# Window attention with graph experts: the first residual added by accumulating transfers, three tasks moved between slots, the sort spread by a new table

## The chip, the cores and the metric

The kernel runs on one core of a Trainium2 chip. A core has engines that run their own instruction queues side by side and wait for each other through semaphores: TensorE (PE, matrix multiply), VectorE (DVE), ScalarE (ACT), GpSimd (POOL) and SyncE (SP, which here only issues transfers). The metric is the time of one execution on the device in microseconds (us), the median of a few runs. Lower is better.

## What is computed

```python
# x: 32 images of 32x32 tokens x 128 features, float32
y = window_attention(layernorm(x))            # 8x8 windows, 8 heads, no mask
y = roll(window_attention(roll(y, (-4, -4)), shift_mask), (4, 4))   # same weights
x = x + y                                      # the residual of this document
t = layernorm(x)                               # 32768 tokens
h = t @ W_gat                                  # 16 graph features a token
# graph attention over 524288 random edges plus one loop a token: a softmax over
# each token's incoming edges gives the scores of 4 experts, the best 2 are taken
out = x + sum_over_top2(gate[e] * (gelu(t @ W1[e] + b1[e]) @ W2[e] + b2[e]))
```

The edges have to be sorted by destination, which the kernel does itself, with compare-and-exchange operations on VectorE over 557,056 keys that lie in SBUF.

## The kernel before

There are three stages, one after the other: `attention` (both window attentions, the layer norm of the result, the graph features, and the whole sort), `edges` (gathers of graph features and the experts), `combine` (gates and sum). Only `attention` is touched.

**Steps and slots.** `attention` is a software pipeline written out by hand. A step is one image for each of two streams: A, the first attention, of image n, and B, the second, of image n-2. There are 39 steps from -2 to 36; streams run in steps 0 to 33. A step has eight slots, one for each pair of windows. In a slot TensorE computes the scores of its pair (lines 929 and 934, by `scores`), transposes those of two slots ago (L948, `turn`), weighs the values of three slots ago (L963, `weigh`), and then does the slot's tasks. It may start the scores of a slot only after VectorE has subtracted the maximum in the slot before (`s_sub`). VectorE takes maximum and subtraction (L1155, L1157, `less_maximum`), then a number of sort operations (L1072 and L1077, smaller and larger), then perhaps statistics of a layer norm (L1061) or a reciprocal (L1145).

**Tasks.** `SLOT_TASKS` lists them by slot. Av/Bv, Ak/Bk and Aq/Bq are value, key and query projections of the streams, FT and CT transposes of normalised images, Ao/Bo transposes of attended values, CH the graph features (L898), and CZ0 and CZ1 the two halves of the result x + attention. `LAG` says how many steps later a task comes for its image. Each task fills one of two PSUM banks (`misc`), taken in turn; ScalarE empties it by a copy. TensorE must wait (`s_free`) until the task two before has been emptied.

**The result.** `result` on TensorE adds three things in the bank: the output bias (one bf16 matmul, L875), the residual `xres` through the identity (L876, 512 columns in float32, shown as one instruction in the program and two in the trace), and attended values times `wo` (L880). ScalarE copies the bank to `x2` (L696). SP loads `xres` once a step (L503) and stores `x2` (L516). VectorE takes the statistics of `x2` in slot 7 (L1061), GpSimd makes mean and deviation of them in 15 linked small instructions (`deviation(1)`, L571 to L585), ScalarE normalises (L738).

**GpSimd** multiplies attended values by the reciprocals of their sums (L601, `normalised_output`) in every second slot, does `deviation(0)` for the input image in slot 4 and `deviation(1)` in slot 7.

**The sort** is one generator of 739 operations. `place_sort` hands them to slots by a credit: `spare(slot)` is what a slot of 7.8 us has left on VectorE after a fixed part, of which the last term comes from a table of eight numbers, one a slot. When a part of the keys has to be transposed, `place_sort` puts turn pieces (tasks S, L911 on TensorE, up to two in a slot, each a bank of 512 or 256 columns) into the slots that follow.

Of the kernel before, what the change touches and what calls it, by code (L numbers as in the profile page):

```python
# [25 lines left out]
P = 128  # L26
# [229 lines left out]
def attention(nc, x, w_qkv, b_qkv, w_o, b_o, w_gat, att_src, att_dst, edge_index, x2_out, tnT_out, node_rows, sorted_keys):  # L256
# [8 lines left out]
    with ExitStack() as ctx:  # L265
# [6 lines left out]
        def sem(name):  # L272
# [24 lines left out]
        xres = sb("xres", [P, TILES, P])  # L297
# [36 lines left out]
        s_xres = sem("s_xres")  # L334
# [35 lines left out]
                      ["CH0", "CZ0"],  # L370
                      ["Bk0", "Bq0", "CZ1"],
# [7 lines left out]
        def spare(slot):  # L379
            k, j = divmod(slot, PAIRS)  # L380
            n = k + FIRST_STEP
            if n < 0:
                return 3.0 if n == -1 and j > 0 else 0.0
            two = LAG["B"] <= n < IMAGES
            busy = (2.5 if two else 1.5) + 0.8
            busy += (0.7, 0.7, 0.7, 0.7, 3.6, -0.6, -0.9, 1.7)[j]
            return SLOT_US - (0.0 if two else 1.5) - busy
# [52 lines left out]
        def _(sp):  # L440
# [49 lines left out]
            for n in steps:  # L490
# [6 lines left out]
                if active("CZ0", n):  # L497
                    m = n - LAG["CZ0"]
                    if m > 0:

                        wait_full(sp, "CZ0", m - 1)
                        wait_full(sp, "CZ1", m - 1)
                    sp.dma_start(xres[:, :, :], x[m].rearrange("(j r) c d -> (r c) j d", j=TILES)).then_inc(s_xres, 16)  # L503
                if active("Ak0", n):
                    own_rows("A", n - LAG["Ak0"], 0)
                if active("CH0", n):
# [3 lines left out]
                if active("Bk0", n):  # L510
                    own_rows("B", n - LAG["Bk0"], 0)
                if active("CZ0", n):
                    m = n - LAG["CZ0"]
                    wait_free(sp, "CZ0", m)
                    wait_free(sp, "CZ1", m)
# [15 lines left out]
        def _(pool):  # L531
# [54 lines left out]

            def normalised_output(n, j):
# [16 lines left out]
            for n in steps:  # L604
                for j in range(PAIRS):
# [3 lines left out]
                    if j == 4 and 0 <= n + 2 < IMAGES:  # L609
                        deviation(0, n + 2)  # L610
                    if j == 7 and active("CZ0", n):
                        deviation(1, n - LAG["CZ0"])
# [199 lines left out]
        def _(pe):  # L812
# [55 lines left out]
            def result(n, task):  # L868
# [5 lines left out]
                pe.wait_ge(s_xres, 16 * m + 16)  # L874
                pe.matmul(t[:, :], all_ones[:, :], osplit[:, :, :].rearrange("p j d -> p (j d)"), start=True, stop=False)  # L875
                pe.matmul(t[:, :], ident[:, :], xres[:, 4 * i:4 * i + 4, :].rearrange("p j d -> p (j d)"), start=False, stop=False)  # L876
# [113 lines left out]
        def _(dve):  # L990
# [169 lines left out]
            for n in steps:  # L1160
                for j in range(PAIRS):
# [14 lines left out]
                    if j == 7 and active("CZ0", n):  # L1176
                        for i in range(2):
                            wait_free(dve, f"CZ{i}", n - LAG["CZ0"])
                        statistics(1, x2, range(TILES), n - LAG["CZ0"])
# [824 lines left out]
```

## Time and profile before

| | |
|---|---|
| time, median of 3 runs | 7,803.55 us (7,803.08 to 7,804.34) |
| the profiled execution | 7,804.57 us, span of its records 7,803.0 us |
| busy over the span | PE 50%, DVE 62%, ACT 27%, POOL 65% |
| mean granted TensorE clock | 0.717 of full speed |
| busy in the attention stage's slices | PE and DVE about nine tenths |

The busy time of an engine is the time in which it executes; waiting for a semaphore is not in it. The shares over the span mix stages: GpSimd leads with the gathers of the second stage, which the change does not touch. Times in the rows below are microseconds from the start of the span. A name such as `attn_keys<-attn_keys` is what is written and what is read, with buffer numbers left out, so that `attn_x` stands for `x2`. An operation of 128x512 in float32 on TensorE appears as two instructions. What ended an idle time stands behind "<-".

### The profile page before, as it was taken

What the parts mean: (1) busy time and instruction counts of PE and PEld (TensorE: products, weight loads), DVE (VectorE), ACT (ScalarE), POOL (GpSimd) and SP (SyncE); (2) the same over time, 40 slices, a digit from 0 to 9 for tenths busy, and PEclk for the clock granted to TensorE, in tenths of its full rate; (3) what the DMA queues carried; (4) which work ended last, traced back from release to release, by engine and by line L of the source; (5) the groups of instructions that cost most, each with busy time, mean ns of one, the idle gap of its engine ahead of it and who ended that gap; (6) DMA issues with size and microseconds to landing.
All of it is one profiled execution on the core that took longest, in us unless ns stands there. A gap on an engine that the chain in (4) does not pass through costs nothing. (4 is left out here: it accounts for less than half of the span.)

```text
span 7803.0 us, 90796 instructions
## 1 busy us (share of the span) xinstructions
PE 3918.8 (50%) x32089; PEld 2498.6 (32%) x32216; DVE 4873.7 (62%) x6373; ACT 2140.2 (27%) x4195; POOL 5082.2 (65%) x5738
## 2 busy tenths in 40 slices
PE   5999999996333433433343343334334333433347
PEld 3666666665212221221222122122212212221123
DVE  9999899997545544554554455455445545544568
ACT  4888888885111111111111111111111111111000
POOL 5443333333777777777777777777777777777674
PEclk9999999998666666666666666666666666666578
DMA  1222222222111211111121111111112111111188
GB/s 51 58 64 57 59 61 60 62 60 71 34 33 33 44 33 33 39 38 33 33 44 33 33 41 36 33 37 40 33 33 44 33 33 39 38 33 33 34 255 278
DMA packets 503676, 417.71 MB, mean 54 GB/s; under 512 B 160546, under 2 KB 400338, under 8 KB 502866
## 3 DMA queue, kind: packets, MB, share of 16 engines
q1 hardware_dynamic: 355842, 356.89, 14.6%
q0 software_dynamic: 147552, 56.96, 7.5%
q8 instruction: 190, 3.11, 0.2%
q14 instruction: 92, 0.75, 0.0%
HBM read 203.44 MB, written 176.45 MB: 49 GB/s over the span
## 5 line engine op out<-in xcount | busy, mean ns | idle before, releaser
L1648 POOL DMA_INDIRECT edge_G<-node_rows,edge_src x4352 | 4126.5, 948 | 1326.3 <-issue 1326.3
L1703 PE MATMUL edge_hbank<-edge_xt,edge_w 128*128 128x512 f32 x1024 | 719.7, 859 | 2755.5 <-ACT edge_hid L1673 2739.5
L1452 DVE TENSOR_TENSOR edge_oh<-edge_wbank,edge_dlf 128x3072 bf16<-128x3072 f32 x512 | 1682.8, 3349 | 62.3 <-PE edge_cbank L1728 46.9
L1409 DVE COPY edge_O<-edge_O 128x24 f32<-128x24 f32 x64 | 12.5, 195 | 2344.7 <-DMA edge_G<-node_rows,edge_src 2344.7
L1703 PEld LDWEIGHTS edge_hbank<-edge_xt,edge_w 128*128 128x128 f32 x1024 | 254.8, 275 | 3184.7 <-ACT edge_hid L1673 3029.3
L1683 ACT ACTIVATE edge_w<-edge_w 128x272 f32<-128x272 f32 x64 | 27.5, 429 | 4043.4 <-DVE edge_w L1423 4043.4
L1728 PE MATMUL edge_cbank<-edge_oh 128*128 128x256 bf16 x4096 | 803.6, 366 | 649.4 <-DVE edge_oh L1452 649.1
L1728 PEld LDWEIGHTS edge_cbank<-edge_oh 128*128 128x128 bf16 x4096 | 477.2, 125 | 952.0 <-DVE edge_oh L1452 814.6
L601 POOL TENSOR_TENSOR attn_att<-attn_oraw,attn_rsum 128x512 f32<-128x512 f32 (+1 forms) x136 | 138.9, 1022 | 952.2 <-DVE attn_rsum L1145 900.3
L1072 DVE TENSOR_TENSOR attn_keys<-attn_keys 128x1024 f32<-128x1024 f32 (+1 forms) x340 | 478.4, 1407 | 9.8
L1077 DVE TENSOR_TENSOR attn_keys<-attn_keys 128x1024 f32<-128x1024 f32 (+1 forms) x340 | 476.8, 1402 | 0.1
L1717 PE MATMUL edge_ybank<-edge_w,edge_hid 128*128 128x128 f32 x4096 | 474.4, 277 | 0.0
L1717 PEld LDWEIGHTS edge_ybank<-edge_w,edge_hid 128*128 128x128 f32 x4096 | 462.2, 192 | 26.1 <-ACT edge_hid L1673 26.1
L1673 ACT ACTIVATE edge_hid<-edge_hbank,edge_b1c 128x512 f32<-128x512 f32 x512 | 344.8, 686 | 255.1 <-PE edge_hbank L1703 254.4
L1155 DVE TENSOR_REDUCE attn_mx<-attn_score 128x16 f32<-128x1024 f32 (+1 forms) x272 | 308.8, 1135 | 106.6 <-PE attn_score L934 67.6
L1157 DVE TENSOR_TENSOR attn_S<-attn_score,attn_mx 128x1024 f32<-128x1024 f32 (+1 forms) x272 | 315.9, 1162 | 9.4
L1845 PE MATMUL comb_total<-comb_ye,comb_ident 128*128 128x512 f32 x512 | 238.8, 630 | 160.5 <-DVE comb_ye L1939 81.8
L929 PE MATMUL attn_score<-attn_km,attn_qT 64*64 64x256 f32 x4096 | 291.9, 399 | 44.5 <-DVE attn_S L1157 35.8
L792 ACT ACTIVATE attn_pT<-attn_turn 128x1024 f32<-128x1024 f32 (+1 forms) x272 | 273.6, 1006 | 93.0 <-PE attn_turn L948 91.6
L963 PE MATMUL attn_out<-attn_vx,attn_pT 128*64 128x34 f32 x8192 | 293.3, 226 | 0.1
L1862 POOL DMA_INDIRECT comb_srow<-state_rows,end_index x256 | 242.1, 946 | 78.1 <-issue 78.1
L948 PE MATMUL attn_turn<-attn_ident,attn_S 128*128 128x128 f32 x2048 | 288.6, 283 | 1.8 <-ACT attn_pT L792 1.8
(282 smaller groups left out, 6465.1 us busy)
## 6 DMA issues: line engine op xcount, KB each, us to landing
edge_G<-node_rows,edge_src POOLq DMA_INDIRECT x4352, 2.4
expert_out<-edge_yo SPq DMA_DIRECT2D x64, 1024.0 KB, 4.3
comb_ye<-expert_out SPq DMA_DIRECT2D x32, 2048.0 KB, 13.6
state_rows<-edge_O SPq DMA_DIRECT2D x64, 816.0 KB
attn_km<-attn_kT SPq DMA_DIRECT2D x1024, 32.0 KB, 2.0
attn_xin<-in_x SPq DMA_DIRECT2D x32, 512.0 KB, 4.3
attn_xres<-in_x SPq DMA_DIRECT2D x32, 512.0 KB, 5.4
x_rows<-attn_x SPq DMA_DIRECT2D x32, 512.0 KB, 3.4
```

The costliest lines, as they stand in the source:

```text
L929: last = pe.matmul(out[2 * e + a], qT[st][h][halves[a], w * WTOK:(w + 1) * WTOK], km[st][halves[a], h, :, w, :], start=True, stop=mask[e] ...
L963: last = pe.matmul(out_bank[e * WTOK:(e + 1) * WTOK, j % OUT_SLOTS, c:c + VW], pT[j % 2][:, st, g, e * WTOK:(e + 1) * WTOK], vx[st][:, 2 * ...
L1072: return dve.tensor_tensor(out, a, b, ALU.min)
L1077: return dve.tensor_tensor(out, a, b, ALU.max)
L1155: dve.tensor_reduce(top, scores, AX_X, ALU.max).then_inc(s_mx, 1)
L1157: dve.tensor_tensor(S[j % RING_S][:, :, lo:hi, :, :].rearrange("p a s h k -> p a (s h) k"), scores, top.unsqueeze(3).to_broadcast([P, 2, ( ...
L1452: dve.tensor_tensor(oh[:, r:r + WIDE, :, :].rearrange("p t k n -> p (t k) n"), iota.unsqueeze(1).to_broadcast([P, 3 * WIDE, P]), dlf[:, t: ...
L1648: pool.indirect_dma_start(G[b][:, t, :], None, node_rows, bass.IndirectOffsetOnAxis(ap=src[b][:, t:t + 1], axis=0)).then_inc(s_g[b][2 * t ...
L1673: act.activation(hid[:, k, :], hbank[k % 2][:, :], ACT.Gelu, bias=b1c[:, k:k + 1]).then_inc(s_ge, 1)
L1703: pe.matmul(hbank[k % 2][:, :], w1[:, k // HB, (k % HB) * P:(k % HB + 1) * P], xt[b][:, :], start=True, stop=True).then_inc(s_l1, 1)
L1717: last = pe.matmul(ybank[:, t, x * P:(x + 1) * P], hid[:, x * HB + h, t * P:(t + 1) * P], w2[:, x, h, :], start=False, stop=(x == EXPERTS ...
L1728: pe.matmul(cbank[:, 0:HI], oh[:, t % RING, 0, :], oh[:, t % RING, 1:3, :].rearrange("p k n -> p (k n)"), start=(t == 0), stop=(t == HC - ...
```

## The change

1. TensorE no longer adds the residual. ScalarE copies bias and projection to `x2` as before; then GpSimd issues two transfers a step, one for each half (`add_residual`, slot 5), that read the image and add it to what stands in `x2` (`accum_op`). VectorE's statistics and SP's store wait for both (`s_added`). `xres` and its load are gone.
2. Slot 5 has Bk0, CZ0, CZ1 (before: CH0, CZ0), slot 6 has Bq0, CH0 (before: Bk0, Bq0, CZ1). SP's transfers follow.
3. The table of `spare` has new numbers.

```diff
-                      ["CH0", "CZ0"],
-                      ["Bk0", "Bq0", "CZ1"],
+                      ["Bk0", "CZ0", "CZ1"],
+                      ["Bq0", "CH0"],
...
-            busy += (0.7, 0.7, 0.7, 0.7, 3.6, -0.6, -0.9, 1.7)[j]
+            busy += (0.85, -0.1, 0.05, 0.2, 3.05, -0.5, 0.55, 2.4)[j]
...
-                    sp.dma_start(xres[:, :, :], x[m].rearrange("(j r) c d -> (r c) j d", j=TILES)).then_inc(s_xres, 16)
                 if active("Ak0", n):
                     own_rows("A", n - LAG["Ak0"], 0)
+                if active("Bk0", n):
+                    own_rows("B", n - LAG["Bk0"], 0)
...
                 if active("CZ0", n):
                     m = n - LAG["CZ0"]
-                    wait_free(sp, "CZ0", m)
-                    wait_free(sp, "CZ1", m)
+                    sp.wait_ge(s_added, 32 * m + 32)
                     sp.dma_start(x2_out[m].rearrange("(j p) d -> p j d", p=P), x2[:, :, :]).then_inc(s_x2st, 16)
...
+            def add_residual(m):
+                rows = x[m].rearrange("(j r) c d -> (r c) j d", j=TILES)
+                for i in range(2):
+                    wait_free(pool, f"CZ{i}", m)
+                    half = slice(TILES // 2 * i, TILES // 2 * (i + 1))
+                    pool.dma_start(x2[:, half, :], rows[:, half, :], accum_op=ALU.add).then_inc(s_added, 16)
...
+                    if j == 5 and active("CZ0", n):
+                        add_residual(n - LAG["CZ0"])
...
-                pe.wait_ge(s_xres, 16 * m + 16)
                 pe.matmul(t[:, :], all_ones[:, :], osplit[:, :, :].rearrange("p j d -> p (j d)"), start=True, stop=False)
-                pe.matmul(t[:, :], ident[:, :], xres[:, 4 * i:4 * i + 4, :].rearrange("p j d -> p (j d)"), start=False, stop=False)
...
-                        for i in range(2):
-                            wait_free(dve, f"CZ{i}", n - LAG["CZ0"])
-                        statistics(1, x2, range(TILES), n - LAG["CZ0"])
+                        m = n - LAG["CZ0"]
+                        dve.wait_ge(s_added, 32 * m + 32)
+                        statistics(1, x2, range(TILES), m)
```

TensorE, slot 5 and the tasks of slot 6 in step 18, before (the score, turn and weigh rows of slot 6 left out; L911 are turn pieces, lines after the change are two lower):

```order
L898 MATMUL attn_misc<-attn_wgat,attn_tnT 128x24 x8
L875 MATMUL attn_misc<-attn_osplit,attn_all_ones 128x512
L876 MATMUL attn_misc<-attn_xres,attn_ident 128x512
L880 MATMUL attn_misc<-attn_wo,attn_attB 128x128 x4
L911 MATMUL attn_misc<-attn_ident,attn_keys 128x128 x8
...
L844 MATMUL attn_misc<-attn_ywin,attn_wfold 128x512 x2
L875 MATMUL attn_misc<-attn_osplit,attn_all_ones 128x512
L876 MATMUL attn_misc<-attn_xres,attn_ident 128x512
L880 MATMUL attn_misc<-attn_wo,attn_attB 128x128 x4
```

and after, the same tasks of slots 5 and 6:

```order
L844 MATMUL attn_misc<-attn_ywin,attn_wfold 128x512
L874 MATMUL attn_misc<-attn_osplit,attn_all_ones 128x512
L878 MATMUL attn_misc<-attn_wo,attn_attB 128x128 x4
L874 MATMUL attn_misc<-attn_osplit,attn_all_ones 128x512
L878 MATMUL attn_misc<-attn_wo,attn_attB 128x128 x4
...
L844 MATMUL attn_misc<-attn_ywin,attn_wfold 128x512
L896 MATMUL attn_misc<-attn_wgat,attn_tnT 128x24 x8
```

The graph features left slot 5 for slot 6, one key projection and the second half of the result went the other way, and the residual is gone; the turn pieces of this step stand in slots 0, 4 and 5 before and in 0, 3 and 4 after.

VectorE, slot 6 of step 18, before (keys are the sort):

```order
L1155 TENSOR_REDUCE attn_mx<-attn_score 128x16
L1157 TENSOR_TENSOR attn_S<-attn_score,attn_mx 128x1024
L1072 TENSOR_TENSOR attn_keys<-attn_keys 128x128x8
L1077 TENSOR_TENSOR attn_keys<-attn_keys 128x128x8
L1072 TENSOR_TENSOR attn_keys<-attn_keys 128x256x4
L1077 TENSOR_TENSOR attn_keys<-attn_keys 128x256x4
L1072 TENSOR_TENSOR attn_keys<-attn_keys 128x512x2
L1145 RECIPROCAL attn_rsum<-attn_oraw 128x32
```

and after:

```order
L1153 TENSOR_REDUCE attn_mx<-attn_score 128x16
L1155 TENSOR_TENSOR attn_S<-attn_score,attn_mx 128x1024
L1075 TENSOR_TENSOR attn_keys<-attn_keys 128x256x4
L1070 TENSOR_TENSOR attn_keys<-attn_keys 128x512x2
L1075 TENSOR_TENSOR attn_keys<-attn_keys 128x512x2
L1143 RECIPROCAL attn_rsum<-attn_oraw 128x32
```

Three sort operations stand in the slot instead of five; slots 1 and 3 have one more each.

GpSimd, from the end of `deviation(0)` in a step to the start of `deviation(1)`, after:

```order
L576 TENSOR_TENSOR attn_nw<-attn_nw 128x8 [waits attn_s_dev]
L583 DMA attn_x<-in_x 128x4x128 [waits attn_s_free1]
L583 DMA attn_x<-in_x 128x4x128 [waits attn_s_free0]
L599 TENSOR_TENSOR attn_att<-attn_oraw,attn_rsum 128x512 [waits attn_s_recip,attn_s_oc]
L562 TENSOR_TENSOR attn_nw<-attn_st 128x8 [waits attn_s_momentc]
```

The two transfers are new; the multiplication of slot 6 (L599, L601 before) now stands behind them.

## Rows read from the trace of the kernel before

**Rows 1.** Windows: stretch, length, busy (count) by engine, granted clock, DMA share, GB/s.

```profile
144.40:557.80 413.40, 374.44 (x5257) 266.16 (x5272) 406.21 (x391) 331.02 (x749) 180.41 (x252) 0.98 0.22 59
557.80:1788.60 1230.80, 1130.53 (x15398) 812.91 (x15444) 1114.43 (x1290) 1011.85 (x2310) 401.81 (x709) 1.00 0.22 59
1881.90:1916.90 35.00, 18.67 (x87) 15.32 (x87) 16.80 (x32) 12.18 (x32) 5.76 (x16) 0.60 0.35 118
```

**Rows 2.** Waits of DVE, 557.8 to 1788.6: total us, times, longest.

```profile
DVE attn_mx L1155 <- PE attn_score L934: 65.3, 44, 4.8
DVE attn_mx L1155 <- PE attn_score L929: 36.7, 26, 5.0
```

**Rows 3.** Timeline of PE, 1016 to 1079: start, length, operation, count, idle before.

```profile
1017.44 1.09 PE L929 MATMUL attn_score<-attn_km,attn_qT 64*64 64x256 f32 x16
...
1050.76 1.23 PE L911 MATMUL attn_misc<-attn_ident,attn_keys 128*128 128x128 f32 x8 [1.58 <-ACT attn_kT L646]
1051.92 1.09 PE L929 MATMUL attn_score<-attn_km,attn_qT 64*64 64x256 f32 x16
...
1057.16 1.02 PE L876 MATMUL attn_misc<-attn_xres,attn_ident 128*128 128x512 f32 x2
1058.02 1.05 PE L880 MATMUL attn_misc<-attn_wo,attn_attB 128*128 128x128 f32 x8
1058.91 0.60 PE L911 MATMUL attn_misc<-attn_ident,attn_keys 128*128 128x128 f32 x4
...
1060.35 1.09 PE L929 MATMUL attn_score<-attn_km,attn_qT 64*64 64x256 f32 x16
...
1067.53 1.09 PE L929 MATMUL attn_score<-attn_km,attn_qT 64*64 64x256 f32 x16
...
1073.16 1.09 PE L929 MATMUL attn_score<-attn_km,attn_qT 64*64 64x256 f32 x16
```

**Rows 4.** Groups by line, PE, 557.8 to 1788.6: busy us, mean ns, idle before.

```profile
L911 PE MATMUL attn_misc<-attn_ident,attn_keys 128*128 128x128 f32 x536 | 85.8, 284 | 52.3 <-ACT attn_vx L656 15.2 <-ACT attn_ywin L684 13.2 <-ACT attn_attB L675 9.6
...
L876 PE MATMUL attn_misc<-attn_xres,attn_ident 128*128 128x512 f32 x88 | 44.9, 592 | 4.5
```

**Rows 5.** Timeline of DVE, 1052 to 1079.

```profile
1053.17 1.22 DVE L1155 TENSOR_REDUCE attn_mx<-attn_score 128x16 f32<-128x1024 f32 x1 [2.15 <-PE attn_score L934]
...
1055.57 1.22 DVE L1072 TENSOR_TENSOR attn_keys<-attn_keys 128x1024 f32<-128x1024 f32 x1
...
1059.10 1.22 DVE L1077 TENSOR_TENSOR attn_keys<-attn_keys 128x1024 f32<-128x1024 f32 x1
...
1074.91 1.64 DVE L1061 BATCH_NORM_STATS2 attn_st<-attn_x 128x6 f32<-128x128 f32 x8
```

**Rows 6.** Timeline of POOL, end of deviation(0) in step 18.

```profile
1059.37 1.00 POOL L584 TENSOR_TENSOR attn_nw<-attn_nw 128x8 f32<-128x8 f32 x1
1060.45 0.20 POOL L585 TENSOR_TENSOR attn_nw<-attn_nw 128x8 f32<-128x8 f32 x1
```

**Rows 7.** Line L1648, gathers of the second stage: durations, and issue to landing.

```profile
L1648 POOL DMA_INDIRECT edge_G<-node_rows,edge_src x4352: 940/944/1505, 1923.8 to 7375.3; - x198
...
DMA to landing us min/median/max: 2.2/2.4/3.3
```

**Rows 8.** DMA issues, 400 to 1600: count, KB each, median us to landing.

```profile
attn_xin<-in_x SPq DMA_DIRECT2D x22, 512.0 KB, 4.4
attn_xres<-in_x SPq DMA_DIRECT2D x22, 512.0 KB, 5.4
```

**Rows 9.** Timelines of ACT, PE, DVE and POOL, end of the stage.

```profile
1883.48 3.20 ACT L738 ACTIVATE attn_normed<-attn_x,attn_nw 128x128 f32<-128x128 f32 x8
...
1883.41 3.61 PE L898 MATMUL attn_misc<-attn_wgat,attn_tnT 128*128 128x24 f32 x16 [1.11 <-ACT attn_attB L675]
...
1893.81 1.64 DVE L1061 BATCH_NORM_STATS2 attn_st<-attn_x 128x6 f32<-128x128 f32 x8 [1.22 <-ACT attn_x L696]
...
1916.86 0.19 POOL L1621 IOTA edge_posi<- 128x68 int32 x1 [14.78 <-POOLq L265]
```

More of the change, by code:

```diff
@@ L296, in attention @@
         normed = sb("normed", [P, TILES, P])
-        xres = sb("xres", [P, TILES, P])
         x2 = sb("x2", [P, TILES, P])
@@ L333, in attention @@
         s_xin = sem("s_xin")
-        s_xres = sem("s_xres")
+        s_added = sem("s_added")
         s_xn = sem("s_xn")
@@ L496, in _ @@
                     load_x(n + 2)
[L497 to L502, printed above, removed]
-                    sp.dma_start(xres[:, :, :], x[m].rearrange("(j r) c d -> (r c) j d", j=TILES)).then_inc(s_xres, 16)
                 if active("Ak0", n):
                     own_rows("A", n - LAG["Ak0"], 0)
+                if active("Bk0", n):
+                    own_rows("B", n - LAG["Bk0"], 0)
                 if active("CH0", n):
@@ L509, in _ @@
                     sp.dma_start(node_rows[m].rearrange("(j p) d -> p j d", p=P), hrow[:, :, :]).then_inc(s_hst, 16)
-                if active("Bk0", n):
-                    own_rows("B", n - LAG["Bk0"], 0)
                 if active("CZ0", n):
                     m = n - LAG["CZ0"]
-                    wait_free(sp, "CZ0", m)
-                    wait_free(sp, "CZ1", m)
+                    sp.wait_ge(s_added, 32 * m + 32)
                     sp.dma_start(x2_out[m].rearrange("(j p) d -> p j d", p=P), x2[:, :, :]).then_inc(s_x2st, 16)
```

## The prediction

> **What bounds the kernel now.** I read the page first: its strip of TensorE is nearly full up to the slice in which the second stage starts, at 1916.86 [rows 9], and a third full from there on. The attention stage is all that the change touches. Then the windows, cut at step borders. In steps 2 to 9 VectorE is busy 406.2 of 413.4 us; in steps 10 to 31 (1,230.8 us) it is busy 1,114.4 and TensorE 1,130.5, at a granted clock of 1.00, the 2.4 GHz level [rows 1]. The waits say who is last. In steps 10 to 31 VectorE stands idle 65.3 + 36.7 = 102 us in 70 of 176 slots, each time for scores [rows 2]. So the early steps are VectorE's, and in the later ones TensorE sets the end of many slots, by 102/22 = 4.6 us a step.
>
> Last the timeline of TensorE in step 18. A slot runs from one group of scores to the next: slot 5 is 1051.92 to 1060.35 = 8.4 us, slot 6 7.2, slot 7 5.6, and the eight from 1017.44 to 1073.16 add to 55.7 [rows 3]. TensorE queues its slot in order (scores, turn, weigh, tasks, turn pieces of the sort), so every microsecond in a task list delays the next scores. Turn pieces (L911) also wait for ScalarE to empty the bank before: the 536 transposes cost 85.8 us busy and 52.3 us idle [rows 4]. A pair in slot 4 of step 18 took 1.23 us and waited 1.58 ahead, 2.8 in all; the one in slot 5 took 1060.35 - 1058.91 = 1.4 [rows 3].
>
> **The change, part by part.**
>
> *Residual matmuls out.* From the start of L876 to that of L880 is 1058.02 - 1057.16 = 0.86 us [rows 3]. There are 88 such instructions, two to a task, in the 22 steps [rows 4]: 44 x 0.86 = 37.8 us off TensorE's queue, and the wait of 4.5 us before them can go too. Upper end of the gain: 42 us. In steps 2 to 9 the same saving (8 x 1.7) lies beside VectorE's work and brings 0.
>
> *Tasks moved.* Bk0 to slot 5, CH0 to slot 6, CZ1 to slot 5. The moved work is unchanged; only the slot sums change. With the base part that a slot has anyway, slot 5 goes from 7.1 to 6.5 us and slot 6 from 7.2 to 6.2 (without turn pieces), since a key projection takes 1.0, the graph features 2.0, a result without its residual 1.1. CZ1 needs the bank of Bk0, which ScalarE can empty only after its four normalisations; by the order of ScalarE in the timeline that is at about the moment TensorE arrives, so I count no wait; if the cover is gone it is 0.3 us a step, 7 us.
>
> *Sort spread anew.* Both programs run 739 sort operations. A steady step has 24 before and after: 3,3,3,3,1,4,5,2 by slot before, 3,4,3,4,1,4,3,2 in step 18 after. One costs (1059.10 - 1055.57)/3 = 1.18 us [rows 5]. VectorE's own sum in a step stays at 51 us, so the spread alone is no gain. It moves the turn pieces: the 67 pairs in steps 10 to 31 stay 67, but 15 of them now fall into slot 4 (8 before) and 10 into slot 3 (6 before), where a pair costs up to the 2.8 us, against 1.4 in slots 5 and 6. I put +4 us on it.
>
> *What VectorE takes back.* I laid both engines side by side slot by slot: scores may not start before the subtraction of the slot before, the maximum not before the scores. In step 18 TensorE's slots add to 55.7 us before (7.3, 6.5, 7.1, 5.8, 7.8, 8.4, 7.2, 5.6) and 54.3 after (7.3, 6.5, 7.1, 8.5, 6.5, 6.5, 6.2, 5.6), VectorE's to 51: 1.4 gained. Thirteen of the 22 steps look like this and give 20 us; in the other nine turn pieces cross a step border or VectorE is later, and they add up to 5. The same working, done for the kernel before, gives 1,224 against the 1,231 of the trace. So -25 us, between 0 (VectorE takes all) and -42.
>
> *The accumulating transfers.* The trace has none, so I bound them. GpSimd issues two per step behind deviation(0), whose last link ends at 1060.45 + 0.2 = 1060.7 in step 18 [rows 6]. In the new order both results are emptied by about 1059.3 (7.4 us behind the scores at 1051.92), so GpSimd is the later one. Issue: a gather of 128 rows holds it for 0.94 us [rows 7]; a half has 512 rows of 512 bytes, by rows four times that, 3.8 us. Landing: 2.4 us for a gather [rows 7], 4.4 and 5.4 us for the plain 512 KB loads of xin and xres [rows 8]; for adding, which reads both sides, at most twice the 5.4. I take 1.2 us per issue and 5.4 to land, from the row that moves the same bytes: the second half is issued at 1061.9 and in at 1067.3. Who waits: VectorE for its statistics in slot 7, which stood at 1074.91 [rows 5]; by its own work alone (slot 5: 7.0, slot 6: 6.3, then 2.4 and two sort operations, from 1053.17) it comes there at 1071.2. Slack 3.9 us, cost 0. With both upper ends (issues end 1064.8 and 1068.9, landing 10.8 later) it is in at 1079.7, some 8 us late. Behind the waiting VectorE stand the next maximum and, one slot on, TensorE's scores. Behind GpSimd's issues stands only the multiplication of slot 6, whose reciprocal comes at about 1065. SP's store of x2 waits too; it stood at 1071 or later anyway, and Bk0's key rows leave SP a slot earlier.
>
> One row bears on GpSimd's pace here: a link of deviation(0) takes 1.00 us where the next takes 0.20 [rows 6], beside sort operations on VectorE. The Trainium skill (SBUF — State Buffer, Who interferes with whom) says that a VectorE instruction with two SBUF inputs contends with a GpSimd instruction that reads SBUF, not with one that only writes it, and infers that descriptor writing is therefore spared. By that rule the issues keep to the price of the gathers; were they held as the reads are, each would wait up to one sort operation, 1.2 us, inside the slack. For the landing only a page has a price: the Trainium skill (DMA: Bandwidth & Descriptors, Anatomy of one DMA — SWDGE (gpsimd) path) gives 2.0 us plus bytes at 436 GB/s for a transfer from GpSimd, an estimate of 2.6 us for 256 KB; by it the half would be in at 1064.5 and the sum the same.
>
> *The end of the stage.* The last image has no cover. Before, its statistics wait for the result copy until 1893.81 and everything up to 1916.86 follows in a chain [rows 9]. After, the graph features (3.61 us from 1883.41, the granted clock being 0.60 in this stretch [rows 1]) stand behind the results and the residual is out, but ScalarE's normalisations until 1886.7 [rows 9] stay in front; both results are then copied by about 1888.9, and with 1.2 + 5.4 us the sum lands near 1895.5. +1 us, between -2 and +12.
>
> Sum: the profiled execution took 7,804.6 us with a span of 7,803.0, and the median of three is 7,803.6, so it stands for them. 7,804.6 - 25 + 1 = 7,780 us.
>
> **Rivals.** (a) *VectorE and the turn pieces take it all back.* For it: VectorE is idle in only 70 of 176 slots [rows 2], and the new table puts 4 operations in slots 1 to 3, where TensorE's tasks are short; a pair in slot 4 waits for ScalarE. With the old TensorE lengths the new spread alone costs 6 us by the working above; if slots 5 and 6 come out 0.5 us longer than I have them, the gain is 4 us. Gain of 0 to 15: 7,790 to 7,805. Against: a wait is 102/70 = 1.5 us long on average, three times that 0.5. (b) *The adding transfer lands late: slower.* Place: VectorE's wait before the x2 statistics. It decides from a landing of 1071.2 - 1061.9 = 9.3 us behind the second issue. At 12 us it is 2.7 late in each of 31 steps; TensorE's remaining lead hides about 1, so 31 x 1.7 = +53, less 25, and 5 at the end: 7,837. At the bound of 8 us late it would be over +150. For it: rows of 512 bytes, reads on both sides, and an issue that may cost 3.8 us. Against: a same-sized plain load needs half of 9.3. (c) *All of it shows*, also ScalarE's shorter waits: -40, 7,764. For it: VectorE's idle time of 4.6 us a step leaves room for all of it.
>
> **How the numbers follow.** Forecast 7,780 (its own range 7,768 to 7,790) 0.50; (c) 0.14; (a) 0.20; (b) 0.16. What this kernel's measurement can tell from no change is about 0.2%, 15.6 us. Below 7,788 lie most of the forecast, all of (c): faster 0.63. Same: the rest of it, (a) and a tenth of (b): 0.23. Slower 0.14. The range takes in (c) and the near part of (b): 7,755 to 7,815.
>
> **What would show it.** Right: the L876 group gone, steps 10 to 31 about 1,206 us, VectorE's wait for scores near 75 us, steps 2 to 9 unchanged, a statistics line (L1059) without idle time. Wrong: idle time before L1059 with the DMA as releaser (b); two slots 3 and 4 longer than 8.5 and 6.5 us (a); DMA landings over 9 us.

## The result, and the profile after

The changed kernel takes 7,827.9 us, median of 9 runs (7,821.5 to 7,830.0); beside it on the same chip the kernel before took 7,803.6 (9 runs). The ratio is 1.0027, 95% interval 1.0016 to 1.0037: slower by 0.27%, where I had forecast 0.3% faster. The profiled execution of after took 7,830.0 us with a span of 7,828.3, against 7,804.6 and 7,803.0 before.

I cut both traces at the first maximum (VectorE, L1153, L1155 before) of each step, and do so for every kernel below. All times are us. "Mult" is where GpSimd's multiplication of slot 6 (L599, L601 before) ends, counted from the start of slot 4, the mean of steps 3 to 9. The ratio is to the kernel before, on the same chip, with its interval. The runs stand on three chips: the kernel before takes 7,803.6 us on that of e1 to e4, 7,812.7 on that of e5 to e8 and 7,813.8 on that of e9 to e12, so times in us compare within these groups, and the ratios across them. Stretches of this stage move less: e7, whose ratio is 1.0001, has 413.4 and 1,230.5 us on the second chip where before has 413.3 and 1,230.8.

```
kernel                      steps 0-1   2-9   10-31   32-33   mult   ratio
before                         76.5   413.3  1230.8    74.2   21.7   1
after                          79.9   441.9  1219.5    76.3   24.6   1.0027 [1.0016, 1.0037]
issues in the chain (e1)       81.2   422.1  1211.9    76.3   22.3   0.9991 [0.9982, 1.0001]
nobody waits (e2)              81.3   444.8  1212.4    76.3   24.8   1.0025 [1.0014, 1.0036]
slots and table only (e3)      81.2   417.1  1235.7    76.8   21.3   1.0020 [1.0010, 1.0029]
after, old table (e4)          76.4   444.8  1219.7    73.7   25.6   1.0027 [1.0017, 1.0036]
nobody waits, issued
  behind the mult (e5)         79.9   417.2  1204.3    74.3   21.2   0.9972 [0.9959, 0.9984]
chain behind the mult (e6)     78.1   416.0  1202.2    76.4   20.7   0.9966 [0.9953, 0.9978]
before, chain behind (e7)      75.2   413.4  1230.5    74.3   21.3   1.0001 [0.9992, 1.0011]
no residual (e8)               81.2   416.8  1204.7    76.3   21.2   0.9969 [0.9957, 0.9980]
four transfers (e9)            79.9   455.1  1250.9    76.3   26.3   1.0082 [1.0065, 1.0099]
long sorts in halves (e10)     80.2   431.1  1214.1    75.7   22.3   1.0010 [1.0000, 1.0019]
transfers only (e11)           76.4   432.6  1245.9    78.7   23.2   1.0043 [1.0026, 1.0060]
e6 with the old table (e12)    76.6   415.5  1221.1    74.2   21.3   0.9986 [0.9977, 0.9996]
```

The loss stands where the prediction had put a zero: steps 2 to 9 grew by 28.6 us, steps 10 to 31 shrank by 11.3 (25 forecast). The last image is no part of the loss: from the last maximum of the stage to the second stage's first IOTA it is 51.2 us, 54.1 before. Of the 25.3 us between the two spans 5.8 lie behind this, in the second and third stages, which the change doesn't touch; they are 5,886 us long in the trace of before, 5,892 in that of after, and 5,886 to 5,899 in the traces of all kernels here. What moves them no run shows. The windows of after, steps 2 to 9 and 10 to 31 (answering to [rows 1]):

```profile
147.40:589.30 441.90, 379.13 (x5243) 271.28 (x5244) 408.11 (x390) 332.19 (x749) 195.77 (x266) 0.94 0.24 55
589.30:1808.90 1219.60, 1106.33 (x15322) 804.60 (x15322) 1119.54 (x1293) 1011.69 (x2308) 452.66 (x753) 0.99 0.26 60
```

VectorE's work in steps 2 to 9 is nearly the same (408.1 us, 406.2 before), in 442 us instead of 413: it waits. TensorE's granted clock in this stretch fell from 0.98 to 0.94. The waits of all engines in steps 2 to 9, 147.4 to 589.3 us: total, times, longest:

```profile
PE attn_misc L865 <- POOL attn_att L599: 35.3, 9, 5.6
...
DVE attn_st L1059 <- DMA attn_x<-in_x: 23.1, 7, 4.8
...
DVE attn_mx L1153 <- PE attn_score L927: 5.7, 5, 2.1
```

and before, 144 to 558 us:

```profile
PE attn_misc L865 <- POOL attn_att L601: 11.9, 6, 4.2
```

Two lines are new or have grown: VectorE waits for the adding transfers before its statistics of x2, and TensorE waits three times as long for GpSimd's multiplication. Which of them costs the time, the list doesn't say. In steps 10 to 31 VectorE's waits for scores went from 102 us [rows 2] to 81.8 (75 forecast):

```profile
DVE attn_mx L1153 <- PE attn_score L932: 48.6, 32, 5.5
DVE attn_mx L1153 <- PE attn_score L927: 33.2, 21, 3.7
DVE attn_st L1059 <- DMA attn_x<-in_x: 5.7, 9, 1.0
```

GpSimd's timeline in step 4 of after, whose slot 4 starts at 281.2 (start, length, instruction):

```profile
289.98 2.31 POOL L567 TENSOR_SCALAR attn_nw<-attn_nw 128x8 f32<-128x8 f32 x1
...
302.20 0.20 POOL L576 TENSOR_TENSOR attn_nw<-attn_nw 128x8 f32<-128x8 f32 x1
302.43 2.68 POOL L583 DMA_DIRECT2D attn_x<-in_x  x2
304.08 2.12 POOL L599 TENSOR_TENSOR attn_att<-attn_oraw,attn_rsum 128x512 f32<-128x512 f32 x1
```

The same place in the kernel before (slot 4 at 271.9):

```profile
278.50 2.31 POOL L576 TENSOR_SCALAR attn_nw<-attn_nw 128x8 f32<-128x8 f32 x1
...
292.52 0.20 POOL L585 TENSOR_TENSOR attn_nw<-attn_nw 128x8 f32<-128x8 f32 x1
292.68 1.05 POOL L601 TENSOR_TENSOR attn_att<-attn_oraw,attn_rsum 128x512 f32<-128x512 f32 x1
```

Before, the multiplication already stood right against the end of deviation(0), 20.8 us after slot 4, and 0.4 us behind its reciprocal. After, the two issues lie between them, and it ends 3.8 us behind the chain instead of 1.0. What that does to TensorE (step 4 of after):

```profile
296.96 1.09 PE L927 MATMUL attn_score<-attn_km,attn_qT 64*64 64x256 f32 x16 [1.99 <-DVE attn_S L1155]
...
306.34 1.94 PE L865 MATMUL attn_misc<-attn_ident,attn_att 128*128 128x128 f32 x8 [5.07 <-POOL attn_att L599]
308.21 1.99 PE L927 MATMUL attn_score<-attn_km,attn_qT 64*64 64x256 f32 x16
```

The transposes of slot 7 start as the multiplication ends (306.20), and the next scores wait behind them. After 5 us of idleness the granted clock is 0.50, the 1.2 GHz level, so the scores take 1.99 us and not 1.09. This isn't new: in the kernel before, TensorE stood idle for 1.88 us at this place, the granted clock was 0.50 behind it as well, and the scores took 1.80 us. What is new in this step is the length of the wait. And VectorE in that step:

```profile
301.35 0.35 DVE L1143 RECIPROCAL attn_rsum<-attn_oraw 128x32 f32<-128x32 f32 x1
...
302.82 1.23 DVE L1155 TENSOR_TENSOR attn_S<-attn_score,attn_mx 128x1024 f32<-128x1024 f32 x1
308.89 0.87 DVE L1059 BATCH_NORM_STATS2 attn_st<-attn_x 128x6 f32<-128x128 f32 x4 [4.85 <-DMA attn_x<-in_x]
```

The reciprocal that the multiplication needs is there at 301.7. Without the issues it would have run from 302.4. The transfers themselves were sized rightly (line L583: issue min/median/max in ns, then to landing in us; 1.2 and 5.4 forecast):

```profile
L583 POOL DMA_DIRECT2D attn_x<-in_x x64: 1290/1367/1882, 246.4 to 1911.1; - x64
...
DMA to landing us min/median/max: 4.4/5.0/7.0
```

### The profile page after: what moved, and what is told of

Its sections match the earlier page's. It is cut to its first block and busy times, and to the rows that moved or that the text cites. A ratio compares the mean times of both kernels' runs of the same rounds, so it can differ in the third digit from the quotient of the medians.

```text
span 7828.3 us, 90571 instructions
## 1 busy us (share of the span) xinstructions
PE 3916.0 (50%) x32088; PEld 2501.9 (32%) x32088; DVE 4877.1 (62%) x6373; ACT 2142.8 (27%) x4195; POOL 5157.1 (66%) x5802
## 5 line engine op out<-in xcount | busy, mean ns | idle before, releaser
L599 POOL TENSOR_TENSOR attn_att<-attn_oraw,attn_rsum 128x512 f32<-128x512 f32 (+1 forms) x136 | 161.8, 1190 | 901.6 <-DVE attn_rsum L1143 815.9
L1715 PEld LDWEIGHTS edge_ybank<-edge_w,edge_hid 128*128 128x128 f32 x4096 | 462.2, 192 | 26.1 <-ACT edge_hid L1671 26.1
L1153 DVE TENSOR_REDUCE attn_mx<-attn_score 128x16 f32<-128x1024 f32 (+1 forms) x272 | 308.8, 1135 | 98.3 <-PE attn_score L932 52.0
L1155 DVE TENSOR_TENSOR attn_S<-attn_score,attn_mx 128x1024 f32<-128x1024 f32 (+1 forms) x272 | 316.0, 1162 | 9.4
## 6 DMA issues: line engine op xcount, KB each, us to landing
comb_ye<-expert_out SPq DMA_DIRECT2D x32, 2048.0 KB, 13.7
```

The source lines that it names most:

```text
L1153: dve.tensor_reduce(top, scores, AX_X, ALU.max).then_inc(s_mx, 1)
L1155: dve.tensor_tensor(S[j % RING_S][:, :, lo:hi, :, :].rearrange("p a s h k -> p a (s h) k"), scores, top.unsqueeze(3).to_broadcast([P, 2, ( ...
L1715: last = pe.matmul(ybank[:, t, x * P:(x + 1) * P], hid[:, x * HB + h, t * P:(t + 1) * P], w2[:, x, h, :], start=False, stop=(x == EXPERTS ...
```

## The experiments

The first theory (A in the expectations) read the larger-looking story: the chain is late, so the transfers land late, so VectorE waits.

**e1, the issues in the middle of the chain.**

```diff
+                if between is not None:
+                    between()
                 link(pool.tensor_tensor(y, v, minus_half[:, :], ALU.pow))
...
                     if j == 4 and 0 <= n + 2 < IMAGES:
-                        deviation(0, n + 2)
-                    if j == 5 and active("CZ0", n):
-                        add_residual(n - LAG["CZ0"])
+                        deviation(0, n + 2, adds)
```

`adds` is `add_residual` of the step's image. Six of the chain's 15 links stand behind the issues, not two as the expectation says.

> As the changed kernel, but GpSimd issues the two adding transfers in the middle of the deviation chain of slot 5 (before its last but one link) instead of behind its end. Theory A (the chain's links are stretched beside VectorE's two-input sort operations, 2.2 us each in steps 2 to 9, so the transfers are issued and land after the time at which VectorE wants to take the statistics of x2): steps 2 to 9 come back from 441.9 us to 413 to 422, slot 7 there from 8.8 to 11.7 us to 7 to 8, VectorE's waits for the transfers in that stretch from 23 us to under 5; total 7785 to 7800. Rival B (adding costs time in itself: the transfers are slow, or disturb others): the waits stay above 15 us and the total at 7820 to 7835. Rival C (the two issues now hold up the chain and what waits for its product): steps 2 to 9 at 430 to 445, the wait now on the query transposes, total 7815 to 7840.

Measured: 7,800.6 us, steps 2 to 9 at 422.1, VectorE's waits for the transfers there 0.9 us, once, slot 7 6.7 us: A's numbers, though the first two are just above its upper ends and slot 7 is below. But the multiplication came earlier too (22.3 us, 24.6 in after), and TensorE's waits for it fell from 35.3 us to 19.0, so the run doesn't tell the two waits apart. In step 4 (slot 4 at 279.3):

```profile
293.49 2.67 POOL L585 DMA_DIRECT2D attn_x<-in_x  x2 [0.30 <-POOL attn_nw L570]
295.14 3.60 POOL L573 TENSOR_TENSOR attn_nw<-attn_nw,attn_minus_half 128x8 f32<-128x8 f32 x1
```

The issues run beside VectorE's sort operations, where a link would have been held up anyway. The chain still ends at 21.5 us, 0.3 later than in after, and the multiplication follows at once: it ends at 22.5 us, 25.0 in after.

**e2, nobody waits for the transfers.** They add into a tile of their own, so the residual is left out of `x2`; the store waits for the copies alone, and GpSimd for the transfers of the step before.

```diff
-                    pool.dma_start(x2[:, half, :], rows[:, half, :], accum_op=ALU.add).then_inc(s_added, 16)
+                    pool.dma_start(spill[:, half, :], rows[:, half, :], accum_op=ALU.add).then_inc(s_added, 16)
...
-                        dve.wait_ge(s_added, 32 * m + 32)
+                        for i in range(2):
+                            wait_free(dve, f"CZ{i}", m)
```

> As the changed kernel, but the two adding transfers go to a tile of their own that nothing reads, and VectorE's statistics and the store wait only for the copies of the output projection: the residual is left out of x2. GpSimd's issues and the bytes stay. Theory A (the cost is VectorE's wait for late transfers): steps 2 to 9 from 441.9 to 413 to 420 us, steps 10 to 31 from 1219.5 to 1205 to 1215, total 7780 to 7797. Rival B (the cost is GpSimd's time for issuing, or what the transfers do to other traffic, or the moved projection): steps 2 to 9 stay at 435 or more, total 7815 to 7830.

Measured: 7,824.8 us, steps 2 to 9 at 444.8. Theory A fell: the wait of 23 us is gone and this stretch is no shorter. (In steps 10 to 31, 1,212.4 us, 7.1 came back.) The waits of this run in steps 2 to 9:

```profile
PE attn_misc L872 <- POOL attn_att L606: 35.2, 9, 6.3
...
DVE attn_mx L1160 <- PE attn_score L934: 27.8, 8, 4.9
```

VectorE now waits 28.7 us for scores (27.8 and one of 0.9); in after it was 29.7 in all, 6.6 for scores and 23.1 for the transfers. TensorE's wait for the multiplication is as long as it was. The wait for the DMA had covered a second one that ends at about the same time: in step 4 of after the scores that stand behind the multiplication end at 310.2, the statistics that stand behind the landing at 310.5. From here on theory F: the two issues stand ahead of the multiplication on GpSimd.

**e3, the moved slots and the new table alone**, the residual still by matmul (SP's order follows the slots, as in the change).

```diff
-                      ["CH0", "CZ0"],
-                      ["Bk0", "Bq0", "CZ1"],
+                      ["Bk0", "CZ0", "CZ1"],
+                      ["Bq0", "CH0"],
...
-            busy += (0.7, 0.7, 0.7, 0.7, 3.6, -0.6, -0.9, 1.7)[j]
+            busy += (0.85, -0.1, 0.05, 0.2, 3.05, -0.5, 0.55, 2.4)[j]
```

> The moved slots and the new spare table of the change alone: both projections in slot 5, graph features in slot 6, but the residual still comes by 88 matmuls with the identity. Theory A (moving costs little, the transfers carry the loss in steps 2 to 9): steps 2 to 9 at 410 to 422 us (before 413.3, changed 441.9), steps 10 to 31 at 1225 to 1240 (TensorE works 1.7 us more per step than in the changed kernel), total 7795 to 7812. Rival D (the move or the table makes the loss): steps 2 to 9 at 435 or more, total 7820 to 7850.

Measured: 7,820.8 us, above A's total and at D's lower edge, though both stretches lie in A's ranges. I had left out steps 0 and 1 (+4.7) and the last two (+2.6). Steps 2 to 9 cost 3.8 us and 10 to 31 4.9, 16 us in all.

**e4, the changed kernel with the old table** (the last two lines of that cut reversed, on the kernel after).

> As the changed kernel with the spare table of the kernel before. Theory A (the table moves only VectorE's share between slots; the late transfers stay): steps 2 to 9 at 432 to 450 us, total 7815 to 7840. Rival E (the new table pushes VectorE's sort operations beside the deviation chain and so makes the transfers late): the chain ends earlier, steps 2 to 9 at 413 to 425, total 7790 to 7805.

Measured: 7,824.6 us, steps 2 to 9 at 444.8: the table doesn't make the loss.

**e5, e2 with the issues behind the multiplication of slot 6.**

```diff
-                    if j == 5 and active("CZ0", n):
+                    if j == 6 and active("CZ0", n):
                         add_residual(n - LAG["CZ0"])
```

> As the run in which nobody waits for the adding transfers (their target is a tile of their own, the residual is left out of x2), but GpSimd issues them in slot 6, behind its multiplication of the attention output, and not ahead of it. Theory F (the loss of steps 2 to 9 is the two issues standing ahead of that multiplication on GpSimd, behind which TensorE's transposes of slot 7 wait): the multiplication ends 21.7 us or less after slot 4's start in steps 3 to 9 (24.8 with the issues ahead of it), steps 2 to 9 from 444.8 us to 413 to 420, total 7785 to 7800. Rival G (the transfers themselves, their bytes or their writing of descriptors, slow the others wherever they are issued): steps 2 to 9 stay at 435 or more, total 7815 to 7828.

Measured: 7,788.7 us, ratio 0.9972, steps 2 to 9 at 417.2: F's numbers. The same instructions and bytes as in e2, behind one instruction more in one queue, and 27.6 us of this stretch are gone. TensorE's wait of 35.2 us fell to:

```profile
PE attn_misc L872 <- POOL attn_att L606: 13.6, 7, 3.2
```

**e8, no residual at all** (neither transfers nor matmuls, otherwise after; `x2` lacks the image).

> The changed kernel without the adding transfers and without the matmuls: the residual is left out of x2 altogether. Beside the kernel with the moved slots and table but the residual by matmul (7820.8) it gives the worth of the 88 removed matmuls alone, beside the changed kernel the whole cost of the transfers. Theory F with VectorE busy 1177 to 1182 us of steps 10 to 31: steps 10 to 31 at 1205 to 1213 (1235.7 with the matmuls), steps 2 to 9 at 412 to 418, total 7783 to 7796. By the prediction's size for the matmuls (0.86 us each, all on the path, 37.8 us in steps 10 to 31) it would be 1198 and 7775 to 7783.

Measured: 7,789.5 us, steps 2 to 9 at 416.8 and 10 to 31 at 1,204.7, within 0.4 us of e5. So adding 256 KB twice a step costs nothing that these stretches show when its issues are out of the way and nobody waits for the landing. Steps 10 to 31 lie 0.3 us below F's range and well above the 1,198 that the prediction's size for the matmuls gave: beside e3 they are worth 31.0 us there, and nothing in 2 to 9. Beside after, the transfers cost 25.1 + 14.8 us.

**e9, four transfers of half the size**, at the place of after.

```diff
-                for i in range(2):
-                    wait_free(pool, f"CZ{i}", m)
-                    half = slice(TILES // 2 * i, TILES // 2 * (i + 1))
+                for i in range(4):
+                    wait_free(pool, f"CZ{i // 2}", m)
+                    part = slice(TILES // 4 * i, TILES // 4 * (i + 1))
...
```

> As the changed kernel, but the same bytes are added by four transfers of two row tiles each instead of two of four. Theory F (each microsecond that GpSimd spends on issues ahead of its multiplication is a microsecond of every step in which the deviation chain ends late): if an issue costs the same whatever it moves (1.4 us), the multiplication of steps 3 to 9 ends 2.7 us later, steps 2 to 9 grow from 441.9 to 460 to 468, steps 10 to 31 by 10 to 35, total 7860 to 7890; if the price goes by the rows described, the four take no longer than the two and the total stays at 7825 to 7835. Rival B (the wait for the landing counts): as the last transfer lands later, a similar loss but with VectorE's waits for the transfers grown above 40 us in that stretch, and no growth of TensorE's wait for the multiplication.

Measured: 7,876.5 us. Waits of this run in its steps 2 to 9, 143.0 to 598.1 us:

```profile
PE attn_misc L865 <- POOL attn_att L599: 45.1, 9, 7.4
...
DVE attn_st L1059 <- DMA attn_x<-in_x: 27.1, 7, 5.9
```

TensorE's wait grew by 9.8 us and VectorE's by 4.0. B wanted over 40 us of the latter and no growth of the former, so it is F and not B. The multiplication ends 1.7 us later than in after, and 8 such steps grew by 13.2 us, 1.65 each; from none to two issues ahead of it (e5 to e2) it is 3.6 us and 27.6/8 = 3.45 each. The extra issues were cheaper than the 2.7 us I gave them (four take 4.99 us in step 4, two 2.68), so steps 2 to 9 came out at 455.1 and not 460 to 468.

**e6, the chain behind the multiplication of slot 6**, everything computed.

```diff
-                    if j == 4 and 0 <= n + 2 < IMAGES:
-                        deviation(0, n + 2)
                     if j == 5 and active("CZ0", n):
                         add_residual(n - LAG["CZ0"])
+                    if j == 6 and 0 <= n + 2 < IMAGES:
+                        deviation(0, n + 2)
```

> As the changed kernel (all computed), but GpSimd's deviation chain for image n+2 moves from slot 4 to slot 6, behind the multiplication; its result is first used in slot 1 of the next step. The adding transfers then have only the multiplication of slot 4 ahead of them. Theory F: issues about 12 us after slot 4's start and landing by 19, multiplication no later than 20 us, no wait of VectorE for the transfers, slot 7 in steps 2 to 9 from 8.95 to 6.0 to 6.6 us, steps 2 to 9 at 412 to 420, steps 10 to 31 at 1205 to 1213, total 7783 to 7796. Rival G (the transfers cost wherever they stand): steps 2 to 9 at 435 or more, total over 7815.

Measured: 7,785.9 us, ratio 0.9966 (0.9953 to 0.9978), steps 2 to 9 at 416.0: F's numbers for time and stretch, steps 10 to 31 (1,202.2) and slot 7 (5.94) a little below them. The multiplication ends at 20.7 us, F had said no later than 20. This version beats both kernels. GpSimd in its step 4 (slot 4 at 272.8):

```profile
279.42 1.06 POOL L599 TENSOR_TENSOR attn_att<-attn_oraw,attn_rsum 128x512 f32<-128x512 f32 x1 [12.07 <-DVE attn_rsum L1143]
281.71 2.69 POOL L583 DMA_DIRECT2D attn_x<-in_x  x2 [1.23 <-ACT attn_x L696]
293.48 1.05 POOL L599 TENSOR_TENSOR attn_att<-attn_oraw,attn_rsum 128x512 f32<-128x512 f32 x1 [9.08 <-DVE attn_rsum L1143]
294.50 0.20 POOL L562 TENSOR_TENSOR attn_nw<-attn_st 128x8 f32<-128x8 f32 x1
```

The transfers go off 8.9 us after slot 4 (21.2 in after, 12 expected), GpSimd then stands idle for 9 us, and the multiplication starts as soon as its reciprocal is there. VectorE is busy 406.2 of the 416.1 us of steps 2 to 9, so little is left to gain there.

**e7, the same move in the kernel before.**

> The kernel before with the same move of the deviation chain behind the multiplication of slot 6, nothing else. Theory F: in steps 2 to 9 the chain already ran into the multiplication in the kernel before (TensorE waited 11.9 us in 6 waits for it in 557.8 us), so steps 2 to 9 fall from 413.3 to 404 to 410 and the total to 7790 to 7800, and the gain of the changed kernel's own version of this move (against the changed kernel) is several times larger. Rival H (the chain's place matters to VectorE's port, not to the multiplication): no more than 3 us either way, 7800 to 7807, or slower if the chain in slots 6 and 7 is held beside the sort operations and makes the next step late.

Measured: ratio 1.0001, steps 2 to 9 at 413.4: no gain, F's 3 to 9 us missed, the rival right. With the chain out of the way the multiplication ends at 21.3 us instead of 21.7. So the chain's end alone had cost nothing: the kernel before stood at the edge, and only what was put behind it counted.

**e10, the long sort operations in halves.**

```diff
-                            yield smaller(low, second, first, factor).then_inc(s_sort, 1)
-                            yield larger(high, second, first, factor).then_inc(s_sort, 1)
+                            o = low.shape[1] // 2
+                            for make, dst in ((smaller, low), (larger, high)):
+                                make(dst[:, :o, :], second[:, :o, :], first[:, :o, :], factor)
+                                yield make(dst[:, o:, :], second[:, o:, :], first[:, o:, :], factor).then_inc(s_sort, 1)
```

> As the changed kernel, but the longest sort operations (2048 elements per partition, 2.28 us each) are issued as two halves. Theory S (the chain's small operations are held until the sort operation beside them ends, so half as long an operation halves the hold): in steps 3 to 9 the chain ends 16 to 18 us after slot 4's start and not 20.1, the multiplication ends at 21 to 22 and not 24.6, and steps 2 to 9 fall from 441.9 to 422 to 435, less the price of the added instructions, which VectorE, full in this stretch, shows in full (about 100 operations at 0.06 us: 6 us). Rival (the chain is held as long whatever the length): chain end within 1 us of 20.1, steps 2 to 9 at 444 to 450. Total 7815 to 7832 by the theory, 7830 to 7840 by the rival.

Measured: 7,822.0 us, ratio 1.0010. The link that took 2.31 us in after takes 1.24:

```profile
286.89 1.24 POOL L567 TENSOR_SCALAR attn_nw<-attn_nw 128x8 f32<-128x8 f32 x1
```

The chain ends at 18.4 us (20.1 in after, 16 to 18 expected), the multiplication at 22.3 (21 to 22 expected), both a little short of S, and steps 2 to 9 at 431.1, inside it. This is why the early steps are the ones that lose: there 92 of 110 sort operations are 2,048 elements long and take 2.3 us, and a link beside one is held until it ends; in steps 10 to 31 508 of 516 are 1,024 long, and the chain of after ends at 16.1 in the mean.

**e11, the transfers alone**, in the slots, order and table of before.

```diff
                     if j == 5 and active("CZ0", n):
-                        add_residual(n - LAG["CZ0"])
+                        add_residual(n - LAG["CZ0"], (0,))
+                    if j == 6 and active("CZ0", n):
+                        add_residual(n - LAG["CZ0"], (1,))
```

> The adding transfers alone: the slots of the kernel before (projections in slots 5 and 6), its order on SyncE and its spare table. The first transfer is issued in slot 5 behind the deviation chain, the second in slot 6 behind the multiplication, once its half is copied. Theory F: one issue instead of two ahead of the multiplication, so steps 2 to 9 at 425 to 432 (before 413.3); the second lands late for the statistics of x2, which VectorE takes in slot 7, so steps 10 to 31 give back their gain: 1215 to 1235; total 7810 to 7830. Rival (the second issue has no room at all: copied only at the end of slot 6, it holds GpSimd and VectorE in every step): 3 to 5 us in each of 30 steps, total 7900 or more.

Measured: 7,846.0 us, between the two ranges; neither sized it. Steps 2 to 9 (432.6) are as F had them within 0.6 us, steps 10 to 31 (1,245.9) are 11 us above. VectorE's waits over the stage:

```profile
DVE attn_st L1061 <- DMA attn_x<-in_x: 48.8, 31, 5.1
```

VectorE waits for a landing in nearly every step. The second half is copied 18.1 us after slot 4 in the mean of steps 10 to 29, and in each of them at least 1.0 us before its issue, which stands behind the multiplication and begins at 22.6: its place in the queue makes it late, more than the copy. TensorE's waits for the multiplication grew as well (20.5 us in 16 waits in steps 10 to 31, 1.1 in 2 before). How the 11 us divide between the two waits no run shows.

**e12, e6 with the old table.**

> The version with the deviation chain behind the multiplication of slot 6, with the spare table of the kernel before instead of the new one. With the chain out of the way the two tables can be compared without the late multiplication. If the new table costs what the stretches of the earlier runs show (3.5 us in steps 2 to 9, 2 to 5 in steps 0 and 1, 2 in steps 32 and 33) and brings nothing in steps 10 to 31: total 7775 to 7783, on a chip on which the new table gives 7786. If it brings VectorE's work to where TensorE leaves room in steps 10 to 31 (5 us or more there): 7784 to 7795.

Measured: 7,802.2 us, ratio 0.9986, outside both ranges: the new table brings 1,221.1 - 1,202.2 = 18.9 us in steps 10 to 31, nearly four times the 5 us that I gave as the least of my larger guess. With the residual on TensorE the moved slots and the table together cost 4.9 (e3), and with the chain in its old place the table was worth 0.2 (e4, 1,219.7, beside 1,219.5). It pays only where TensorE has been relieved and the multiplication isn't late. The old table leaves 8.8 of 23.2 sort operations a step in slots 5 and 6, where VectorE then sets the end (7.61 and 8.51 us a slot in e12, 7.61 and 8.56 in before; with 4.8 sort operations of 1.2 us, the maximum, the subtraction and the reciprocal, slot 6 is full). The reciprocal comes last in slot 6, and the multiplication waits for it: TensorE's waits for the multiplication in steps 10 to 31 are 18.6 us in 15 with the old table, 3.4 in 4 in e6. So the microseconds taken from TensorE bring only 9.7 there.

## Why the prediction was wrong

- **The issues' cover: the step that failed.** "Behind GpSimd's issues stands only the multiplication of slot 6, whose reciprocal comes at about 1065", and the sum has no term for it, in any step. The sentence names the right instruction; its slack I had read in step 18 alone. There the chain ended 15.0 us after slot 4 and the multiplication began 9.75 us behind it. In steps 3 to 9 of the same trace the chain ended at 20.6, and the multiplication began 0.0 us behind it. The transfers cost 25.1 us in steps 2 to 9 and 14.8 in 10 to 31 (e8 to after). In 2 to 9 it is the issues' place (e2, e5). In 10 to 31 steps 15, 17 and 21 have a late chain in after too and lose 3.2 to 4.1 us each, TensorE's waits for the multiplication there are 13.7 us (3.4 in e8), and about half of the 14.8 may be the landing (7.1, e2). Without these 39.9 us the profiled execution would stand at about 7,790.
- **Rival (b)** was slower, with its place at the landing and a wait before the statistics; I gave it 0.16. The sign was its, the mechanism for the most part wasn't: the wait that it names showed up (23.1 us in steps 2 to 9), and taking it away (e2) gave nothing there and 7.1 us in steps 10 to 31. The landing stayed under 9.3 us in after (7.0 at most).
- **Residual matmuls out.** 37.8 us in steps 10 to 31 were put down, 31.0 came (e3 to e8). Right that steps 2 to 9 get nothing.
- **The sum for steps 10 to 31**, -25 without the transfers' cost: e8 gives 1,204.7 - 1,230.8 = -26.1. Right in sum, and in part by luck: "Thirteen of the 22 steps look like this", 1.4 us each, isn't what came. Steps 28 to 31 alone give 12.2 of the 26.1, and six steps (12, 16, 19, 23, 24, 27) got longer by 0.5 to 2.2. TensorE's slot 5 came out at 7.3 us in the mean of steps 11 to 26 (6.5 forecast, the shortest 6.66), slot 6 at 6.2 (6.2).
- **Turn pieces and rival (a).** The spread and the moved slots together cost 4.9 us in steps 10 to 31 with the residual still on TensorE (e3); +4 and "6 us" were put on the spread. That fits, though no run has the spread alone on TensorE's old lengths. But I gave it 0 in the other steps; there it cost 3.8 in 2 to 9 and some 7 in the first and last two.
- **Transfers.** Issue 1.37 us (1.2), landing 5.0 (5.4): right. The estimate of 2.6 us that the prediction took from the Trainium skill (DMA: Bandwidth & Descriptors, Anatomy of one DMA — SWDGE (gpsimd) path) is too short: none in after landed in under 4.4 us, and the measured time stands. The upper ends were added up wrong by a little: two issues of 3.8 us behind 1060.7 end at 1064.5 and 1068.3, not 1064.8 and 1068.9; nothing hangs on it.
- **Stage end** -2.9 (+1, between -2 and +12): just outside.
- **The Trainium skill's rule on who interferes** (SBUF — State Buffer, Who interferes with whom), that descriptor writing is spared what GpSimd's reads suffer beside two-input VectorE instructions: the trace agrees, no issue of after took over 1.88 us, and in e9 the record of the fourth issue is 2.7 us long whether a sort operation ran beside it (steps 5 to 8) or not (steps 4 and 9), while links beside the 2.3 us sorts took up to 2.31. I had used it for the issues only. It speaks as much of the chain ahead of them: a link of 0.20 us is held until the sort operation beside it ends, which I had at 1.2 us and which is 2.3 in the early steps.

## What to carry to other kernels

Slack is read at its tightest step, not at a typical one: before putting work into an in-order queue, list for each step the distance between the end of what stands before it and the start of what stands behind it (here 9.75 us in step 18, 0 in steps 3 to 9). A wait in the list is not yet a cost: two waits may cover each other, and only a run without the one tells. A move that frees one engine may pay in full only if the work of its partner is spread anew at the same time (steps 10 to 31: 9.7 us with the old table, 28.6 with the new one, both with the late chain), so try such parts together as well as apart.

## What the runs showed of the hardware

- An adding transfer of 256 KB in rows of 512 bytes from GpSimd: 1.37 us to issue, two in a row 2.7, four of half the size 5.0, landing after 5.0 us (4.4 to 7.0). The 16.8 MB of both halves over 32 images made neither stretch more than 0.4 us longer (e5 against e8). In three steps of after (10, 18 and 25) GpSimd stood idle for 3.6 to 3.9 us between the two issues, and in three of e6 for 3.9, with nothing shown that it waited for.
- The record of GpSimd's multiplication is 2.12 us long behind the issues and 1.05 without them; the mean in steps 2 to 9 went from 1,030 to 1,414 ns. In step 4 of after the record starts 1.03 us before that of the second issue ends (at 305.11) and ends 1.09 us behind it, while VectorE stands idle: the multiplication itself is no slower there. Where a sort operation of 2,048 elements ran beside it (steps 5, 7, 8), the record is 3.07 us long.
- A link of the chain (8 elements a partition) beside a VectorE operation with two inputs lasts until that one ends: up to 2.31 us beside 2,048 elements, 1.24 beside 1,024 (e10), 0.20 alone (1.67 for the power). In after 210 links of over 0.5 us, the power left out, end a median of 0.06 us behind the end of such an operation.
